# The read of one group of eight moved from GpSimd to VectorE, its states kept in PSUM, and the replicated buffers turned by halves

## The chip, the cores and the metric

The kernel runs on one core of one Trainium2 chip. The metric is the device time of one launch in microseconds. Five engines work side by side: TensorE (PE, with its weight loads PEld), VectorE (DVE), ScalarE (ACT), GpSimd (POOL) and SyncE (SP), which issues most of the transfers.

## The reference

For each of 32 sequences of 256 time steps and 128 features the kernel computes a selective state-space block and then a mixture-of-experts block, both with a layer norm ahead and a residual. Cut to what matters here, for each sequence:

```
uo = norm(x) @ W_in.T ; u, o = halves of uo ; u = silu(conv(u))       # 256 channels
g = u @ W_gate.T -> delta_lo (64), b (16), c (16)
delta = softplus(delta_lo @ W_delta.T + bias) ; A = -exp(A_log)
h[t] = exp(A * delta[t]) * h[t-1] + (delta[t] * u[t]) * b[t]          # 256 channels x 16 states
y[t] = sum over states of h[t] * c[t] ; y = (y + D * u) * silu(o) ; x = x + y @ W_out.T
x = x + experts(norm(x))    # router, top 2 of 8, silu(x wg) * (x wu) wd, and a shared expert
```

## The kernel before

**The scan.** One sequence has 256 channels x 16 states. They are cut into eight groups (`q` from 0 to 7; `half` of the channels is `q // 4`, four states `g` are `q % 4`), and each group is a tile of 128 partitions x 4 blocks x 256 time steps, so 128x1024. For each group:

- `decays` on ScalarE (L451): four Exp activations from the replicated delta (`rep[..., 0, :]`) into `decay_ps`, a PSUM tensor of two slots used in turn (`at % 2`);
- `inject_group` on GpSimd (L384): the replicated delta times u, times b, into `inject` (four slots);
- `scan` on VectorE (L648): one scan along the 1024 columns, decays and injections in, `state` (three slots) out. Column 0 of each block in `decay_ps` is kept at zero, which starts each block anew;
- `read_group` on GpSimd (L393): `state` times c into `read` (three slots);
- `sum_states` on TensorE (L856): four matmuls with `sum_sel` that add the products over states into `y_ps`.

**What feeds it.** `dd` holds delta (copied by ScalarE, L536, from PSUM) and delta times u (VectorE, L780); eight DMAs of SP (L330), four for each half of the channels, replicate it to `rep`. A buffer `rep[n % 2]` holds both halves, so there are four halves of space in all. b and c come by two DMAs into `bc`.

**The order.** The kernel is a software pipeline: `steps(body)` calls, on each engine, `body(k, on)` for k from -3 to 34, and in step k the scan of sequence k runs beside the expert block of sequence k-2 (`f`), the first layer norm and convolution of sequence k+2, and delta and replication of sequence k+1. Each engine runs its own program in order, written out by hand, and waits on semaphores. VectorE has, in a step: scan(0), scan(1), the small operations of the router, scan(2), the low part of xnT (L769), scan(3), scan(4), then `dd` (L780, which waits for `delta_mm`, the matmul L991), then `gated_up(4)` and so on. GpSimd has injects 1 to 3, reads 0 and 1, inject 4, reads 2, 3 and 4, injects 5 to 7, inject 0 of the next sequence, the small `shift` (L414), reads 5 to 7. TensorE's `ups(4, f)` (L1007, its matmuls at L873) waits for `dd_done`, since `delta_ps` and the bank of `ups(4)` are the same PSUM bank. ScalarE copies `dd` only when VectorE's L780 is done:

```
act.wait_ge(du_done, n + 1)
...
act.copy(dd[:, :, 0, :], delta_ps).then_inc(dd_done, 1)
...
pe.wait_ge(dd_done, k + 2)
...
ups(4, f)
```

Of the kernel before, what the change touches and what calls it, by code (L numbers as in the profile page):

```python
# [5 lines left out]
ALU = mybir.AluOpType  # L6
# [5 lines left out]
P = 128  # L12
# [7 lines left out]
CB = P // GS  # L20
# [18 lines left out]
SCALE = 2.5  # L39
LOW = 32  # L40

RX, RU, RI, RS, RR = 5, 3, 4, 3, 3


GATE_BANK = [0, 2, 1, 0, 1, 1, 0]
# [5 lines left out]

def rows(chunk):
    return LAST if chunk == NSH - 1 else P


def comb_chunks(i):
# [4 lines left out]
def build(nc, x, W_in, conv_w, conv_b, W_gate, W_delta, delta_bias, A_log, Dskip, W_out,  # L61
          gate_w, w_gate, w_up, w_down, sw_gate, sw_up, sw_down, out):
    with ExitStack() as ctx:
        def sb(name, shape, dt=F32):
            return ctx.enter_context(nc.sbuf_tensor(name, shape, dt))

        def sem(name):
            return ctx.enter_context(nc.semaphore(name))
# [1 line left out]
        features = sb("features", [P, CHUNKS, T])  # L70
        state = sb("state", [P, RS, JB, T])
        read = sb("read", [P, RR, JB, T])
        rep = [sb(f"rep{i}", [P, HALVES * JB, 2, T]) for i in range(2)]

        scratch = features[:].rearrange("p c t -> p (c t)")
        wconv_rows = scratch[:, 0:1024].rearrange("p (c k d) -> p c k d", c=HALVES, k=TAPS)
# [148 lines left out]
        inject_done = sem("inject_done")  # L225
        state_done = sem("state_done")
        read_done = sem("read_done")
        sum_done = sem("sum_done")
        y_taken = sem("y_taken")

# [52 lines left out]
        def count(value):  # L283
            return max(value, 0)
# [13 lines left out]
        @block.sync  # L298
        def _(sp):
            sp.dma_start(x_in[0][:], x_t[0]).then_inc(x_loaded[0], 16)  # L300
            for to, source in setup_loads:
                sp.dma_start(to, source).then_inc(w_loaded, 16)

            def body(k, on):
                if on(1):
                    n = k + 1
                    sp.wait_ge(bc_out, 16 * (n + 1))
                    sp.wait_ge(inject_done, count(GROUPS * k))
                    sp.wait_ge(read_done, count(GROUPS * k))
                    for which, landed in enumerate((b_in, c_in)):  # L310
                        rows_of = bc_dram[:, which, :, :].rearrange("s g t -> s (g t)")
                        sp.dma_start(bc[n % 2][:, which, :, :].rearrange("p g t -> p (g t)"),
                                     rows_of.unsqueeze(0).broadcast_to([CB, GS, SG * T])).then_inc(landed, 16)
                if on(-3):
                    n = k - 3
                    sp.wait_ge(result_done, n + 1)
                    sp.dma_start(out_t[n], result[n % 2][:]).then_inc(stored[n % 2], 16)
                if on(4):

                    n = k + 4  # L320
                    sp.wait_ge(x1_done, count(n - RX + 1))
                    sp.dma_start(x_in[n % RX][:], x_t[n]).then_inc(x_loaded[n % RX], 16)
                if on(1):
                    n = k + 1
                    sp.wait_ge(dd_done, n + 1)
                    sp.wait_ge(decay_done, count(GROUPS * k))
                    for half in range(HALVES):
                        for j in range(JB):
                            source = dd[j * CB:(j + 1) * CB, half, :, :].rearrange("c w t -> c (w t)")
                            sp.dma_start(rep[n % 2][:, half * JB + j, :, :].rearrange("p w t -> p (w t)"),  # L330
                                         source.unsqueeze(1).broadcast_to([CB, GS, 2 * T])).then_inc(rep_in[half], 16)
# [12 lines left out]
        def _(pool):  # L344
# [30 lines left out]
            def body(k, on):  # L375
                def inject_group(n, q):
                    half, g = divmod(q, SG)
                    at = GROUPS * n + q
                    pool.wait_ge(rep_in[half], 16 * JB * (n + 1))
                    pool.wait_ge(b_in, 16 * (n + 1))  # L380
                    pool.wait_ge(state_done, count(at - RI + 1))
                    du_all = rep[n % 2][:, half * JB:(half + 1) * JB, 1, :]
                    b_all = bc[n % 2][:, 0, g, :].unsqueeze(1).broadcast_to([P, JB, T])
                    pool.tensor_tensor(inject[:, at % RI], du_all, b_all, ALU.mult).then_inc(inject_done, 1)  # L384

                def read_group(n, q):
                    half, g = divmod(q, SG)
                    at = GROUPS * n + q
                    pool.wait_ge(c_in, 16 * (n + 1))
                    pool.wait_ge(state_done, at + 1)  # L390
                    pool.wait_ge(sum_done, count(at - RR + 1))
# [12 lines left out]

                injects(1, 2, 3)
                reads(0, 1)
                injects(4)
                reads(2, 3, 4)
                injects(5, 6, 7)
                if on(1):  # L410
                    inject_group(k + 1, 0)
                if on(3) or on(-1):
                    pool.wait_ge(ln_rstd, k + 4)
                    pool.tensor_tensor(shift[:], neg_mean[:], rstd[:], ALU.mult).then_inc(ln_shift, 1)  # L414
                reads(5, 6, 7)
# [4 lines left out]
        def _(act):  # L420
# [14 lines left out]
            def body(k, on):  # L435
# [8 lines left out]
                def decays(n, q):  # L444
                    half, g = divmod(q, SG)
                    at = GROUPS * n + q
                    act.wait_ge(rep_in[half], 16 * JB * (n + 1))
                    act.wait_ge(state_done, count(at - 1))
                    for j in range(JB):
                        col = (g * HALVES + half) * JB + j  # L450
                        last = act.activation(decay_ps[:, at % 2, j, 1:T], rep[n % 2][:, half * JB + j, 0, 1:T], ACT.Exp,  # L451
                                              scale=neg_a[:, col:col + 1])
                    last.then_inc(decay_done, 1)

# [145 lines left out]
        def _(dve):  # L600
# [39 lines left out]
            def body(k, on):  # L640
                f = k - 2

                def scan(q):
                    at = GROUPS * k + q
                    dve.wait_ge(decay_done, at + 1)
                    dve.wait_ge(inject_done, at + 1)
                    dve.wait_ge(read_done, count(at - RS + 1))
                    dve.tensor_tensor_scan(state[:, at % RS].rearrange("p j t -> p (j t)"),  # L648
                                           decay_ps[:, at % 2].rearrange("p j t -> p (j t)"),
                                           inject[:, at % RI].rearrange("p j t -> p (j t)"), 0.0,  # L650
                                           ALU.mult, ALU.add).then_inc(state_done, 1)

                def gated_up(p):
                    at = PAIRS * f + p
# [171 lines left out]
        def _(pe):  # L826
# [18 lines left out]
            def body(k, on):  # L845
                f = k - 2

                def sum_states(n, q):
                    half, g = divmod(q, SG)
                    at = GROUPS * n + q  # L850
                    if g == 0:
                        pe.matmul(y_ps, skip[:, half, :], u[n % RU][:, half, :], start=True, stop=False,
                                  skip_group_check=True)
                    pe.wait_ge(read_done, at + 1)
                    for j in range(JB):
                        last = pe.matmul(y_ps[j * CB:(j + 1) * CB, :], sum_sel[:], read[:, at % RR, j, :],  # L856
                                         start=False, stop=(g == SG - 1), skip_group_check=True)
                    last.then_inc(sum_done, 1)

# [263 lines left out]
```

## Time and profile before

| what | value |
|---|---|
| median of 3 runs | 1453.29 us (1452.8 to 1456.53) |
| the profiled execution, its own time | 1453.74 us |
| its span from first to last instruction | 1451.6 us |
| busy share of the span | PE 88%, PEld 65%, DVE 72%, ACT 74%, POOL 84% |
| a step in the steady part | about 41.5 us |
| TensorE's granted clock, mean | 0.961 of full speed |

An engine's busy share is an average over the whole span; start and end, where the pipeline fills and empties, are in it. The time of a launch is a little longer than the span in the trace. Times in the rows are in us from the start of the span, and the name in brackets behind a row is what ended the engine's idle time before it.

### The profile page before, as it was taken

The page shows a single profiled execution, that of the slowest core. Times are in us where ns is not written, and L with a number is a line of the kernel's source. Part 1 is how long each engine was busy: PE and PEld are TensorE (multiplying, and loading weights), DVE is VectorE, ACT ScalarE, POOL GpSimd, SP SyncE. Part 2 cuts the span into 40 slices and gives each one's busy share as a digit, 9 for nine tenths or more (in the row PEclk, how much of TensorE's full clock was granted, in tenths as well). Part 3 has the DMA queues.
Part 4 walks back from the last instruction along what each step waited for, and adds up shares of the span by engine and source line. Part 5 has one row for each costly group of instructions (what it writes and reads, how often), then busy time and mean ns, then how long its engine had stood idle before and what let it go on. Part 6 is the DMA issues. An engine that isn't in the chain of part 4 may idle for free.

```text
span 1451.6 us, 26176 instructions
## 1 busy us (share of the span) xinstructions
PE 1273.9 (88%) x9203; PEld 950.7 (65%) x9203; DVE 1042.5 (72%) x1664; ACT 1080.1 (74%) x2219; POOL 1219.0 (84%) x568
## 2 busy tenths in 40 slices
PE   3455999999999999999999999999999999998888
PEld 2223766777667667776676677766766777665677
DVE  2245778877777788777777887777778877776753
ACT  3777778777877787778777877787778777876642
POOL 3299898898889988988899889888998898899920
PEclk8667999999999999999999999999999999999989
DMA  3433322333333223333332233333322333233000
GB/s 102 103 89 84 92 67 69 95 96 92 74 86 95 65 70 96 96 93 75 84 94 66 70 96 96 92 74 85 95 65 69 96 97 92 69 83 89 7 5 8
DMA packets 71486, 115.08 MB, mean 79 GB/s; under 512 B 8174, under 2 KB 30396, under 8 KB 71356
## 3 DMA queue, kind: packets, MB, share of 16 engines
q1 hardware_dynamic: 67180, 110.71, 30.2%
q10 hardware_dynamic: 4176, 2.70, 0.6%
q8 instruction: 73, 1.20, 0.3%
q14 instruction: 57, 0.47, 0.1%
HBM read 41.04 MB, written 5.24 MB: 32 GB/s over the span
## 4 chain that ended last, share of the span: by engine, by line
PE 34%; DVE 22%; ACT 17%; issue 16%; POOL 1%; DVEq 0%; SPq 0%; DMA 0%; ACTq 0%; POOLq 0%
DVE state L648 11%; PE work_ps L864 10%; PE work_ps L873 10%; ACT decay_ps L451 6%; DVE features L666 5%; PE acc_ps L898 4%; ACT L483 3%; ACT L504 3%; PE acc_ps L856 3%; ACT L548 3%; PE work_ps L1081 2%; PE work_ps L997 2%; PE work_ps L927 2%; ACT u L526 2%; DVE features L658 2%
## 5 line engine op out<-in xcount | busy, mean ns | idle before, releaser
L393 POOL TENSOR_TENSOR read<-state,bc 128x1024 f32<-128x1024 f32 x256 | 605.6, 2379 | 93.0 <-DVE state L648 87.6
L384 POOL TENSOR_TENSOR inject<-rep,bc 128x1024 f32<-128x1024 f32 x256 | 604.4, 2385 | 52.2 <-DMA rep<-dd 52.2
L648 DVE TENSOR_TENSOR_SCAN state<-decay_ps,inject 128x1024 f32<-128x1024 f32 x256 | 580.9, 2280 | 48.3 <-ACT decay_ps L451 29.5
L451 ACT ACTIVATE decay_ps<-rep,neg_a 128x255 f32<-128x255 f32 x1024 | 423.5, 462 | 14.6 <-DVE state L648 5.5
L442 ACT ACTIVATE g_silu<-work_ps 128x512 f32<-128x512 f32 x224 | 133.9, 598 | 204.3 <-PE work_ps L864 204.0
L658 DVE TENSOR_TENSOR features<-g_silu,work_ps 128x512 f32<-128x512 f32 x224 | 151.6, 678 | 147.5 <-PE work_ps L873 107.5
L898 PE MATMUL acc_ps<-ffn_down,features 128*128 128x128 f32 (+1 forms) x1792 | 252.5, 284 | 0.0
L898 PEld LDWEIGHTS acc_ps<-ffn_down,features 128*128 128x128 f32 (+1 forms) x1792 | 217.2, 191 | 30.1 <-issue 12.3
L864 PE MATMUL work_ps<-xn2T_part,ffn_gate 128*128 128x256 f32 x1344 | 210.9, 294 | 2.5 <-ACT combT L499 1.8
L873 PE MATMUL work_ps<-xn2T_part,ffn_up 128*128 128x256 f32 x1344 | 207.7, 291 | 1.4 <-ACT dd L536 1.4
L856 PE MATMUL acc_ps<-read,sum_sel 128*32 128x256 f32 x2048 | 168.3, 401 | 37.8 <-POOL read L393 37.6
L873 PEld LDWEIGHTS work_ps<-xn2T_part,ffn_up 128*128 128x128 f32 x1344 | 180.5, 195 | 27.4 <-ACT dd L536 13.6
L864 PEld LDWEIGHTS work_ps<-xn2T_part,ffn_gate 128*128 128x128 f32 x1344 | 180.6, 196 | 17.4 <-issue 13.1
L666 DVE TENSOR_TENSOR features<-features,work_ps 128x512 f32<-128x512 f32 (+1 forms) x192 | 113.9, 630 | 18.1 <-PE work_ps L885 18.1
L979 PE MATMUL work_ps<-xnT_part,wconv 128*128 128x256 f32 x768 | 103.2, 292 | 26.7 <-DVE xnT_part L769 26.7
L979 PEld LDWEIGHTS work_ps<-xnT_part,wconv 128*128 128x128 f32 x768 | 96.5, 194 | 37.2 <-DVE xnT_part L769 36.4
L856 PEld LDWEIGHTS acc_ps<-read,sum_sel 128*32 128x32 f32 x2048 | 40.8, 109 | 110.0 <-POOL read L393 49.2
L885 PE MATMUL work_ps<-combT,csel 40*128 40x256 f32 x352 | 87.4, 334 | 2.0 <-DVE features L658 2.0
L474 ACT ACTIVATE gate<-work_ps 128x512 f32<-128x512 f32 x32 | 19.1, 596 | 66.8 <-PE work_ps L927 66.8
L885 PEld LDWEIGHTS work_ps<-combT,csel 40*128 40x128 f32 x352 | 53.4, 185 | 20.4 <-DVE features L658 2.8
L927 PE MATMUL work_ps<-xnT_part,wo 128*128 128x256 f32 x192 | 32.3, 305 | 34.4 <-DVE features L658 30.7
L780 DVE TENSOR_TENSOR dd<-work_ps,u 128x512 f32<-128x512 f32 x32 | 22.1, 691 | 48.9 <-PE work_ps L991 48.9
(134 smaller groups left out, 1398.5 us busy)
## 6 DMA issues: line engine op xcount, KB each, us to landing
rep<-dd SPq DMA_DIRECT2D x256, 256.0 KB, 4.8
bc<-bc_rows SPq DMA_DIRECT2D x64, 512.0 KB, 4.8
x_in<-in_L_attn_x_dram SPq DMA_DIRECT2D x32, 128.0 KB, 2.2
out_dram<-result SPq DMA_DIRECT2D x32, 128.0 KB, 1.8
bc_rows<-g_sb SPq DMA_DIRECT2D x32, 32.0 KB
state<-in_L_ffn_w_gate_dram ACTq DMA_DIRECT2D x1, 704.0 KB, 4.4
read<-in_L_ffn_w_up_dram ACTq DMA_DIRECT2D x1, 704.0 KB, 5.9
ffn_down<-in_L_ffn_w_down_dram ACTq DMA_DIRECT2D x1, 704.0 KB, 7.1
```

The lines of the kernel that those rows point to most:

```text
L384: pool.tensor_tensor(inject[:, at % RI], du_all, b_all, ALU.mult).then_inc(inject_done, 1)
L393: pool.tensor_tensor(read[:, at % RR], state[:, at % RS], c_all, ALU.mult).then_inc(read_done, 1)
L451: last = act.activation(decay_ps[:, at % 2, j, 1:T], rep[n % 2][:, half * JB + j, 0, 1:T], ACT.Exp, scale=neg_a[:, col:col + 1])
L648: dve.tensor_tensor_scan(state[:, at % RS].rearrange("p j t -> p (j t)"), decay_ps[:, at % 2].rearrange("p j t -> p (j t)"), inject[:, at ...
L658: dve.tensor_tensor(features[:, 2 * p:2 * p + 2, :].rearrange("p c t -> p (c t)"), g_silu[p % 2][:], banks[UP_BANK[p]][:], ALU.mult).then_ ...
L666: dve.tensor_tensor(to, to, banks[COMB_BANK[i]][:, 0:len(chunks) * T], ALU.mult).then_inc(hc_done, 1)
L856: last = pe.matmul(y_ps[j * CB:(j + 1) * CB, :], sum_sel[:], read[:, at % RR, j, :], start=False, stop=(g == SG - 1), skip_group_check=True)
L864: last = pe.matmul(banks[GATE_BANK[p]][:, side * T:(side + 1) * T], ffn_gate[w][:, chunk * P:(chunk + 1) * P], xn2T_parts[n % 2][d][:], st ...
L873: last = pe.matmul(banks[UP_BANK[p]][:, side * T:(side + 1) * T], ffn_up[w][:, chunk * P:(chunk + 1) * P], xn2T_parts[n % 2][d][:], start= ...
L885: last = pe.matmul(banks[COMB_BANK[i]][:, at * T:(at + 1) * T], csel[:, (chunk - NSH) * P:(chunk - NSH + 1) * P], combT[:], start=True, st ...
L898: last = pe.matmul(down_ps[:, j * DIM:(j + 1) * DIM], features[0:r, chunk, j * P:(j + 1) * P], ffn_down[0:r, chunk, :], start=fresh and j ...
L979: last = pe.matmul(conv_ps[:, half * T:(half + 1) * T], wconv[w][:, half, tap, :], xnT_parts[d][:, tap:tap + T], start=(w + d + tap == 0), ...
```

## The change

Group 4 (`OWN`), the fifth of each sequence, is treated apart. Its scan writes its states in place over its decays in `decay_ps`, not into `state`. VectorE, not GpSimd, multiplies them by c into a new tile `read_own` (128x1024), and then sets column 0 of the slot's four blocks to zero again with a memset. `sum_states` of this group takes `read_own`. The decays of group 6, which use the same slot, wait for the memset. GpSimd reads only seven groups, and the slots of `state` and `read` are counted over these seven (`others`, `of_others`). The replicated buffers are three of one half each, in turn, in place of two of both halves; the DMAs of each half wait for the decays and injections that used its buffer.

```
-RX, RU, RI, RS, RR = 5, 3, 4, 3, 3
+RX, RU, RI, RS, RR, RP = 5, 3, 4, 3, 3, 3
+OWN = 4
+OTHERS = GROUPS - 1
...
+def others(n, q):
+    return OTHERS * n + (q if q < OWN else q - 1)
+def of_others(at):
+    n, q = divmod(at, OTHERS)
+    return GROUPS * n + (q if q < OWN else q + 1)
...
-        rep = [sb(f"rep{i}", [P, HALVES * JB, 2, T]) for i in range(2)]
+        read_own = sb("read_own", [P, JB, T])
+        rep = [sb(f"rep{i}", [P, JB, 2, T]) for i in range(RP)]
...
                     sp.wait_ge(dd_done, n + 1)
-                    sp.wait_ge(decay_done, count(GROUPS * k))
                     for half in range(HALVES):
+                        sp.wait_ge(decay_done, count(SG * (HALVES * n + half - RP + 1)))
+                        sp.wait_ge(inject_done, count(SG * (HALVES * n + half - RP + 1)))
...
-                reads(2, 3, 4)
+                reads(2, 3)
...
-                    act.wait_ge(state_done, count(at - 1))
+                    if q == OWN + 2:
+                        act.wait_ge(decay_zero, n + 2)
+                    else:
+                        act.wait_ge(state_done, count(at - 1))
...
-                    dve.wait_ge(read_done, count(at - RS + 1))
-                    dve.tensor_tensor_scan(state[:, at % RS].rearrange("p j t -> p (j t)"),
-                                           decay_ps[:, at % 2].rearrange("p j t -> p (j t)"),
+                    decays = decay_ps[:, at % 2].rearrange("p j t -> p (j t)")
+                    if q == OWN:
+                        to = decays
+                    else:
+                        dve.wait_ge(read_done, count(others(k, q) - RS + 1))
+                        to = state[:, others(k, q) % RS].rearrange("p j t -> p (j t)")
+                    dve.tensor_tensor_scan(to, decays,
                                            inject[:, at % RI].rearrange("p j t -> p (j t)"), 0.0,
                                            ALU.mult, ALU.add).then_inc(state_done, 1)
+
+                def read_own_group():
+                    dve.wait_ge(c_in, 16 * (k + 1))
+                    dve.wait_ge(state_done, GROUPS * k + OWN + 1)
+                    dve.wait_ge(sum_done, count(GROUPS * (k - 1) + OWN + 1))
+                    c_all = bc[k % 2][:, 1, OWN % SG, :].unsqueeze(1).broadcast_to([P, JB, T])
+                    dve.tensor_tensor(read_own[:], decay_ps[:, OWN % 2], c_all, ALU.mult).then_inc(read_own_done, 1)
+                    dve.wait_ge(read_own_done, k + 1)
+                    dve.memset(decay_ps[:, OWN % 2, :, 0:1], 0.0).then_inc(decay_zero, 1)
...
                 if on(0):
                     scan(4)
+                    read_own_group()
...
-                    pe.wait_ge(read_done, at + 1)
+                    if q == OWN:
+                        pe.wait_ge(read_own_done, n + 1)
+                        products = read_own
+                    else:
+                        pe.wait_ge(read_done, others(n, q) + 1)
+                        products = read[:, others(n, q) % RR]
```

VectorE's order in the middle of a steady step, before (L648 is a scan, L769 the low part of xnT, L780 the product for `dd`):

```order
L761 TENSOR_TENSOR comb_parts<-work_ps,comb_parts 128x2x8 [waits comb_split]
L648 SCALAR_TENSOR_TENSOR state<-decay_ps,inject 128x1024 [waits read_done,inject_done,decay_done]
L769 TENSOR_TENSOR xnT_part<-work_ps,xnT_part 128x256 [waits xnT_high]
L648 SCALAR_TENSOR_TENSOR state<-decay_ps,inject 128x1024 [waits read_done,inject_done,decay_done] x2
L780 TENSOR_TENSOR dd<-work_ps,u 128x2x256 [waits rep_in1,rep_in0,delta_mm]
L658 TENSOR_TENSOR features<-g_silu,work_ps 128x512 [waits down_mm,ffu_mm,silu_done]
```

The same place of the changed kernel, whose lines are numbered anew (L675 is the scan, L684 the product with c, L686 the memset, L816 the product for `dd`):

```order
L796 TENSOR_TENSOR comb_parts<-work_ps,comb_parts 128x2x8 [waits comb_split]
L675 SCALAR_TENSOR_TENSOR state<-decay_ps,inject 128x1024 [waits read_done,inject_done,decay_done]
L804 TENSOR_TENSOR xnT_part<-work_ps,xnT_part 128x256 [waits xnT_high]
L675 SCALAR_TENSOR_TENSOR state<-decay_ps,inject 128x1024 [waits read_done,inject_done,decay_done]
L675 SCALAR_TENSOR_TENSOR decay_ps<-decay_ps,inject 128x1024 [waits inject_done,decay_done]
L684 TENSOR_TENSOR read_own<-decay_ps,bc 128x1024 [waits sum_done,state_done,c_in]
L686 MEMSET decay_ps 128x4 [waits read_own_done]
L816 TENSOR_TENSOR dd<-work_ps,u 128x2x256 [waits rep_in1,rep_in0,delta_mm]
```

Two instructions now stand between scan(4) and the product for `dd`, and each of them waits for the one ahead of it.

GpSimd's order over one step, before (L384 is an inject, L393 a read):

```order
L384 TENSOR_TENSOR inject<-rep,bc 128x1024 [waits state_done,b_in,rep_in1]
L393 TENSOR_TENSOR read<-state,bc 128x1024 [waits sum_done,state_done,c_in] x3
L384 TENSOR_TENSOR inject<-rep,bc 128x1024 [waits state_done,b_in,rep_in1] x3
L384 TENSOR_TENSOR inject<-rep,bc 128x1024 [waits state_done,b_in,rep_in0]
L414 TENSOR_TENSOR shift<-neg_mean,rstd 128x4 [waits ln_rstd]
```

And of the changed kernel (L403 is an inject, L412 a read):

```order
L403 TENSOR_TENSOR inject<-rep,bc 128x1024 [waits state_done,b_in,rep_in1]
L412 TENSOR_TENSOR read<-state,bc 128x1024 [waits sum_done,state_done,c_in] x2
L403 TENSOR_TENSOR inject<-rep,bc 128x1024 [waits state_done,b_in,rep_in1] x3
L403 TENSOR_TENSOR inject<-rep,bc 128x1024 [waits state_done,b_in,rep_in0]
L433 TENSOR_TENSOR shift<-neg_mean,rstd 128x4 [waits ln_rstd]
```

The third of the reads behind inject 4 is gone, and the three injects and all behind them follow one operation sooner.

## Rows read from the trace of the kernel before

**Rows 1.** The page's part 1, busy time and share of each engine.

```profile
PE 1273.9 (88%) x9203; PEld 950.7 (65%) x9203; DVE 1042.5 (72%) x1664; ACT 1080.1 (74%) x2219; POOL 1219.0 (84%) x568
```

**Rows 2.** Busy time by stretch: length, PE, PEld, DVE, ACT, POOL, clock, DMA.

```profile
815.00:1230.00 415.00, 387.01 (x2872) 290.42 (x2871) 320.83 (x510) 326.86 (x680) 377.70 (x171) 1.00 0.33 84
```

**Rows 3.** The page's part 4, shares of the chain that ended last, by engine.

```profile
PE 34%; DVE 22%; ACT 17%; issue 16%; POOL 1%; DVEq 0%; SPq 0%; DMA 0%; ACTq 0%; POOLq 0%
```

**Rows 4.** Timeline of GpSimd over one step: start, length, operation, idle before.

```profile
633.87 2.36 POOL L384 TENSOR_TENSOR inject<-rep,bc 128x1024 f32<-128x1024 f32 x1 [0.60 <-DMA rep<-dd]
...
639.46 2.37 POOL L393 TENSOR_TENSOR read<-state,bc 128x1024 f32<-128x1024 f32 x1 [0.74 <-DVE state L648]
...
660.50 7.22 POOL L393 TENSOR_TENSOR read<-state,bc 128x1024 f32<-128x1024 f32 x3 [1.25 <-DVE state L648]
667.66 7.08 POOL L384 TENSOR_TENSOR inject<-rep,bc 128x1024 f32<-128x1024 f32 x3
675.40 2.37 POOL L384 TENSOR_TENSOR inject<-rep,bc 128x1024 f32<-128x1024 f32 x1 [0.66 <-DMA rep<-dd]
```

**Rows 5.** The chain in order of time, same step: start, length, what.

```profile
658.07 2.30 DVE state L648
...
666.56 1.10 PE work_ps L997 x4
667.66 0.91 PE work_ps L873 x6
...
675.13 0.04 DVE state L648
```

**Rows 6.** Timeline of all engines from 665 to 668.3, same step.

```profile
662.79 2.26 DVE L648 TENSOR_TENSOR_SCAN state<-decay_ps,inject 128x1024 f32<-128x1024 f32 x1
...
666.23 0.69 DVE L780 TENSOR_TENSOR dd<-work_ps,u 128x512 f32<-128x512 f32 x1 [1.18 <-PE work_ps L991]
...
666.95 0.58 ACT L536 COPY dd<-work_ps 128x512 f32<-128x512 f32 x1
...
667.59 0.77 PEld L873 LDWEIGHTS work_ps<-xn2T_part,ffn_up 128*128 128x128 f32 x6 [0.36 <-ACT dd L536]
```

**Rows 7.** Waits over the whole span: us in total, times, longest.

```profile
DVE dd L780 <- PE work_ps L991: 48.9, 32, 5.6
...
PEld work_ps L873 <- ACT dd L536: 13.6, 29, 3.0
```

**Rows 8.** Timeline of VectorE, same step: a shorter product, and three operations in a row.

```profile
648.36 0.42 DVE L672 TENSOR_TENSOR y_gated<-acc_ps,gate 128x256 f32<-128x256 f32 x1 [0.23 <-PE acc_ps L856]
...
657.76 0.17 DVE L759 CAST comb_parts<-work_ps 128x16 fp32r<-128x16 f32 x1
657.97 0.17 DVE L761 TENSOR_TENSOR comb_parts<-work_ps,comb_parts 128x16 fp32r<-128x16 f32 x1
658.07 2.29 DVE L648 TENSOR_TENSOR_SCAN state<-decay_ps,inject 128x1024 f32<-128x1024 f32 x1
```

**Rows 9.** The instructions of one line: the memset of decay_ps, min/median/max ns.

```profile
L638 DVE MEMSET decay_ps<- x1: 65/65/65, 21.3 to 21.3; 128x8 f32 x1
```

**Rows 10.** Timeline of VectorE: a product written to PSUM, and one written to SBUF.

```profile
644.55 0.29 DVE L813 TENSOR_TENSOR work_ps<-logit,work_ps 128x128 f32<-128x128 f32 x1
644.75 0.28 DVE L815 TENSOR_TENSOR ahead<-logit,work_ps 128x128 f32<-128x128 f32 x1
```

**Rows 11.** Timeline of SP's queue, same step.

```profile
667.56 8.92 SPq L330 DMA_DIRECT2D rep<-dd  x8
```

**Rows 12.** Timelines of the first and the last steps, VectorE's L780.

```profile
87.81 0.69 DVE L780 TENSOR_TENSOR dd<-work_ps,u 128x512 f32<-128x512 f32 x1 [4.49 <-PE work_ps L991]
...
1330.04 0.69 DVE L780 TENSOR_TENSOR dd<-work_ps,u 128x512 f32<-128x512 f32 x1 [1.51 <-PE work_ps L991]
```

**Rows 13.** Timeline of GpSimd at the end of step 0.

```profile
96.80 2.35 POOL L384 TENSOR_TENSOR inject<-rep,bc 128x1024 f32<-128x1024 f32 x1 [1.94 <-DMA rep<-dd]
```

**Rows 14.** Timeline of ScalarE, same step: the decays of group 3.

```profile
658.04 1.66 ACT L451 ACTIVATE decay_ps<-rep,neg_a 128x255 f32<-128x255 f32 x4
```

More of the change, by code:

```diff
@@ L227, in build @@
         read_done = sem("read_done")
+        read_own_done = sem("read_own_done")
         sum_done = sem("sum_done")
@@ L308, in body @@
                     sp.wait_ge(inject_done, count(GROUPS * k))
-                    sp.wait_ge(read_done, count(GROUPS * k))
+                    sp.wait_ge(read_done, count(OTHERS * k))
+                    sp.wait_ge(read_own_done, count(k))
                     for which, landed in enumerate((b_in, c_in)):
@@ L325, in body @@
                     sp.wait_ge(dd_done, n + 1)
-                    sp.wait_ge(decay_done, count(GROUPS * k))
                     for half in range(HALVES):
+                        sp.wait_ge(decay_done, count(SG * (HALVES * n + half - RP + 1)))
+                        sp.wait_ge(inject_done, count(SG * (HALVES * n + half - RP + 1)))
                         for j in range(JB):
                             source = dd[j * CB:(j + 1) * CB, half, :, :].rearrange("c w t -> c (w t)")
-                            sp.dma_start(rep[n % 2][:, half * JB + j, :, :].rearrange("p w t -> p (w t)"),
+                            sp.dma_start(rep[(HALVES * n + half) % RP][:, j, :, :].rearrange("p w t -> p (w t)"),
                                          source.unsqueeze(1).broadcast_to([CB, GS, 2 * T])).then_inc(rep_in[half], 16)
@@ L381, in inject_group @@
                     pool.wait_ge(state_done, count(at - RI + 1))
-                    du_all = rep[n % 2][:, half * JB:(half + 1) * JB, 1, :]
+                    du_all = rep[(HALVES * n + half) % RP][:, :, 1, :]
                     b_all = bc[n % 2][:, 0, g, :].unsqueeze(1).broadcast_to([P, JB, T])
@@ L387, in read_group @@
                     half, g = divmod(q, SG)
[L388 removed]
+                    at = others(n, q)
                     pool.wait_ge(c_in, 16 * (n + 1))
[L390 to L391 removed]
+                    pool.wait_ge(state_done, GROUPS * n + q + 1)
+                    pool.wait_ge(sum_done, count(of_others(at - RR) + 1))
                     c_all = bc[n % 2][:, 1, g, :].unsqueeze(1).broadcast_to([P, JB, T])
@@ L447, in decays @@
                     act.wait_ge(rep_in[half], 16 * JB * (n + 1))
-                    act.wait_ge(state_done, count(at - 1))
+                    if q == OWN + 2:
+                        act.wait_ge(decay_zero, n + 2)
+                    else:
+                        act.wait_ge(state_done, count(at - 1))
                     for j in range(JB):
                         col = (g * HALVES + half) * JB + j
-                        last = act.activation(decay_ps[:, at % 2, j, 1:T], rep[n % 2][:, half * JB + j, 0, 1:T], ACT.Exp,
+                        last = act.activation(decay_ps[:, at % 2, j, 1:T], rep[(HALVES * n + half) % RP][:, j, 0, 1:T], ACT.Exp,
                                               scale=neg_a[:, col:col + 1])
@@ L853, in sum_states @@
                                   skip_group_check=True)
-                    pe.wait_ge(read_done, at + 1)
+                    if q == OWN:
[4 more added lines that the diff above has]
+                        products = read[:, others(n, q) % RR]
                     for j in range(JB):
-                        last = pe.matmul(y_ps[j * CB:(j + 1) * CB, :], sum_sel[:], read[:, at % RR, j, :],
+                        last = pe.matmul(y_ps[j * CB:(j + 1) * CB, :], sum_sel[:], products[:, j, :],
                                          start=False, stop=(g == SG - 1), skip_group_check=True)
```

## The prediction

> **What bounds the kernel now.** I read the busy shares first, then the steady part by itself, then the chain that ended last, then one step engine by engine.
>
> Over the whole span TensorE is busy 88% and GpSimd 84% [rows 1]. In a steady stretch of 415 us, ten steps, PE is busy 387.0, POOL 377.7, ACT 326.9 and DVE 320.8 us, at the full clock [rows 2]. A step is 675.40 - 633.87 = 41.5 us, read between two injects of the same place [rows 4]. So GpSimd is busy 37.8 of 41.5 us, and by shares alone one would say that it is nearly the limit, and that one 2.36 us read taken from it must pay.
>
> The chain says otherwise: GpSimd has 1% of it; PE has 34%, DVE 22%, ACT 17% [rows 3]. The timeline of GpSimd shows why: its 3.7 us of idle time in a step end, each time, on a scan of VectorE or on a DMA of `rep` [rows 4]. In the steady part I found no engine that waits for GpSimd long enough to move its own work. GpSimd follows; it does not lead.
>
> What leads is a loop through three engines. In one step [rows 5]: VectorE's scan(2) at 658.07, ScalarE's table loads and u, TensorE's g matmuls (L997) at 666.56, `ups(4)` (L873) at 667.66, the gate and up matmuls behind it, ScalarE's last silu, table load and decays, scan(5) at 675.13; from there scans, router and expert matmuls lead back to the next scan(2). TensorE works without a gap from `ups(4)` to the last silu's matmuls, so a late `ups(4)` makes all of it late.
>
> The place to look at is just ahead of `ups(4)` [rows 6]. scan(4) ends at 662.79 + 2.26 = 665.05. VectorE idles 1.18 us for the matmul L991 and runs L780 from 666.23 to 666.92. ScalarE's copy (L536) starts at 666.95, 0.03 us later, and ends at 667.53. The weight load of `ups(4)` starts at 667.59, ended by that copy. L997's matmuls end at 667.66 by the chain, and matmuls overlap their forerunner by about 0.07 us, so the matmul was free to start at 667.59 too. **The two paths into `ups(4)` are level: what makes L780 late makes the step late.** It is so in nearly all steps: PEld's wait for this copy is counted 29 times [rows 7].
>
> **The change part by part.**
>
> *GpSimd loses one read of about 2.36 us in each step.* It comes behind inject 4. Injects 5 to 7, from 667.66 to 674.74, move forward by 2.4 us, but the next inject waits for `rep`, already now until 675.40 [rows 4]. Its transfers start at 667.56, when `dd` is done [rows 11], and don't move forward. So the 2.4 us become idle time there, 3.0 us in place of 0.66. Gain: nothing. In step 0, where the pipeline fills, the inject of the same place already waits 1.94 us [rows 13]; nothing there either.
>
> *VectorE gains three things between scan(4) and L780*: the wait for the scan, the product, the wait for the product and the memset. 1.18 us of idle time cover them; the question is whether this is enough.
> - The product, 128x1024, one operand in PSUM: no row has this size. 128x256 takes 0.42 [rows 8], 128x512 takes 0.69 [rows 6], so 0.27 for each 256 columns and 0.69 + 2 x 0.27 = 1.23 for 1024. Upper bound two of 512, 1.38.
> - A wait for the operation just ahead: L759 ends at 657.93 and L761, which waits for it, starts at 657.97, a gap of 0.04 [rows 8]. Operations that don't wait start before the forerunner ends: L761 ends at 658.14, the scan behind it starts at 658.07, 0.10 us after L761 started. Two such waits are added: 0.04 each, upper bound 0.10.
> - The memset: 0.065 us for 8 columns [rows 9], here 4. L780 doesn't wait for it and starts between 0.03 and 0.10 us after it; the nearest row has 0.10 [rows 8] behind a longer operation, and I take 0.09. Upper bound 0.17, the length of a small operation [rows 8].
>
> Sum: 665.05 + 0.04 + 1.23 + 0.04 + 0.09 = 666.45. L780 started at 666.23, so it is **0.22 us late**. Its output releases the copy, the copy `ups(4)` and the DMAs of `rep`. What is late next is the whole loop, 0.22 us in each step.
>
> *How many steps.* L780 waits 32 times for 48.9 us [rows 7]. Step 0 has 4.49 us of cover, the last one (step 30) 1.51 [rows 12], more than the 1.40 added. Steps 2 to 29 are alike, 28 of them. 28 x 0.22 = 6.2 us. Lower bound of the sum: with the gap behind scan(4) and the product alone, 665.05 + 0.04 + 1.23 = 666.32, 0.09 late, 2.5 us. Upper bound: 665.13 + 0.10 + 1.38 + 0.10 + 0.17 = 666.88, 0.65 late, 18 us (the scan's 0.08 is below).
>
> *The scan into PSUM, in place*: a product of 128 columns written to PSUM takes 0.29, one written to SBUF 0.28 [rows 10]. I take no difference; by this row 1024 columns could cost 0.08. No row shows a scan written to PSUM.
>
> *The wait of decays 6 for the memset*: the memset ends at about 666.4, the decays start at 675 or later. Covered by 8 us. *scan(4) no longer waits for a read*: it did not wait before. *PE's `sum_states` of group 4*: product ready at 666.3, taken at 674. Free.
>
> *The three halves of `rep`.* Half 0 of the next sequence goes to the buffer of the sequence before's second half, long read. Half 1 goes where the running sequence's half 0 lay: it needs decays 0 to 3 and injects 0 to 3. Decays 3 end at 659.70 [rows 14], the DMAs start at 667.56 [rows 11] and those of half 1 some 4 us later. Cover 8 us and more; cost nothing. Without that cover the replication would wait, and inject 0 and read 5 behind it.
>
> *A rule against my sum.* The rows show that a wait costs: a start 0.04 us after the forerunner's end in place of 0.07 before it [rows 8], 0.11 us for each of two waits, and this is my 0.22 us. The Trainium skill, page "VectorE: DVE Perf Modes", section "The DRAIN you can't avoid", says that between VectorE operations "the semaphore costs nothing extra". By it the sum would be 666.23 and the delay nothing. The row shows the contrary, though on small operations; a rival below takes this in.
>
> **The total.** 1453.74 (the profiled execution's own time) + 6.2 = 1459.9. That execution is 0.45 us above the median of the runs, so against the median: 1459.5 us, 0.4% slower.
>
> **The rivals.** A measurement of this kernel tells a difference from none at about 0.3%, 4.4 us.
> - *The added work just fits.* If the waits overlap as operations without waits do, L780 starts within 0.05 us of its old time and the time stays at 1453.3 to 1455. For it: the margin is a fifth of a microsecond and every term is short. Against: the gap of 0.04 us. With it go the lower bound above (0.09 us, 1455.8) and all delays up to 0.155 us: 35%.
> - *The scan in place is dear.* 2.26 us for 1024 columns is 2.2 ns each, two reads or so per column. If reading and writing one PSUM bank made it half slower, scan(4) would grow by 1.1 us, L780 be 1.3 us late, the time 1453 + 28 x 1.3 = 1490. Against: the 0.01 us of [rows 10]. With milder forms, up to the upper bound of 18 us and beyond: 11%.
> - *Faster: GpSimd is the limit after all.* It is busy 91% of a step [rows 2]. If the scans that it waits for themselves wait for it through a path that the chain hides, a step could shrink by up to the 2.4 us removed: 28 x 2.4 = 67 us, 1386. It decides once the loop through the scans is shorter than GpSimd's own 37.8 us; the loop would have to lose 3.7 us first, and the change takes nothing from it. 6%.
> - *The forecast*, L780 0.155 to 0.4 us late in each step, 1457.7 to 1464.5: 48%.
>
> **The numbers.** Slower by over 0.3%: 48 + 11 = 59%. Within 0.3%: 35%. Faster: 6%. The range from 1453 to 1467 holds the forecast, the case that fits, and the milder half of the dear scan; outside are the 6% faster and the dearest scans, and what is shifted by chance at the lower edge. The forecast's own range is 1457.7 to 1464.5.
>
> **What would show it.** Right: the step is 41.7 us; the product's row has about 1.23 us; VectorE's idle time ahead of the `dd` product, 1.18 before, is gone, while PEld's wait for the copy of `dd` grows by 0.2 us a time; GpSimd's wait for `rep` grows from 0.66 to about 3 us; GpSimd's busy time falls by 32 x 2.4 = 76 us with no gain in time. Wrong: some idle time left ahead of the `dd` product (it fits), a scan to PSUM well over 2.28 us (dear), or a step under 41.5 us (GpSimd). It would also be wrong if TensorE could start `ups(4)` with slack that the modelled ends of matmuls hide.

## The result and the profile after

The changed kernel takes 1461.48 us in the median (16 runs, 1457.69 to 1467.27), the kernel before on the same chips 1454.9 us (16 runs, 1450.6 to 1460.43). The ratio is 1.0052, 95% interval 1.0035 to 1.0069: slower by half a per cent, which is 7.6 us; the two medians differ by 6.6. 1459.5 us and 0.4% were forecast.

Between launches of one kernel the time spreads over 10 us, more than the effect, and in the traces it is mostly the filling and the last steps that vary. A finer measure is the length of one step in the steady part, from one `dd` product of VectorE to the next. Inside the trace of the changed kernel 26 of the 27 steps from 3 to 29 agree within 0.03 us and one is 0.34 longer; in that of the kernel before all but two agree within 0.05, and these are 0.23 and 0.39 longer. The median over these steps is 41.473 us before and 41.766 us after, 0.29 us more. This is the number that the experiments below compare.

The page of the changed kernel, part 1:

```profile
PE 1277.7 (88%) x9203; PEld 951.6 (65%) x9203; DVE 1084.3 (74%) x1728; ACT 1078.0 (74%) x2219; POOL 1144.2 (78%) x536
```

GpSimd lost 75 us of work, VectorE got 42, and the span went from 1451.6 to 1459.1. The timeline of the place just ahead of `ups(4)`, which answers to [rows 6] (L675 is the scan, L684 the product with c, L686 the memset, L816 the product for `dd`, L558 ScalarE's copy, L914 `ups(4)`):

```profile
623.96 2.27 DVE L675 TENSOR_TENSOR_SCAN decay_ps<-decay_ps,inject 128x1024 f32<-128x1024 f32 x1
...
626.33 1.23 DVE L684 TENSOR_TENSOR read_own<-decay_ps,bc 128x1024 f32<-128x1024 f32 x1
...
627.63 0.06 DVE L686 MEMSET decay_ps<- 128x4 f32 x1
627.70 0.69 DVE L816 TENSOR_TENSOR dd<-work_ps,u 128x512 f32<-128x512 f32 x1
...
628.42 0.59 ACT L558 COPY dd<-work_ps 128x512 f32<-128x512 f32 x1 [0.25 <-DVE dd L816]
...
629.06 0.77 PEld L914 LDWEIGHTS work_ps<-xn2T_part,ffn_up 128*128 128x128 f32 x6 [0.65 <-ACT dd L558]
629.06 0.98 PE L914 MATMUL work_ps<-xn2T_part,ffn_up 128*128 128x256 f32 x6 [0.22 <-ACT dd L558]
```

Read it from the top. scan(4) ends at 626.23. The `dd` product starts at 627.70, 1.46 us later by the unrounded times, where it was 666.23 - 665.05 = 1.18 before. VectorE no longer waits for the matmul that makes delta (L991 before); its 1.18 us of idle time are used up and 0.28 us more. ScalarE now waits 0.25 us for the product, and TensorE, which had no gap here, 0.22 us for the copy. The step is longer by 0.29.

The waits over the whole span say the same, as answers to [rows 7]:

```profile
POOL inject L403 <- DMA rep<-dd: 132.7, 32, 26.6
...
PEld work_ps L914 <- ACT dd L558: 21.5, 29, 3.0
...
ACT dd L558 <- DVE dd L816: 11.9, 32, 1.5
PE work_ps L914 <- ACT dd L558: 7.9, 29, 1.4
```

TensorE itself has a wait of 7.9 us in 29 steps, 0.27 each in the mean, but 0.22 in nearly all of them and 1.4 in one. And GpSimd's wait for `rep` is 132.7 us, where it was 52.2 before. The first line is that of the kernel before, the second one step now, against [rows 4], where it was 0.66:

```profile
POOL inject L384 <- DMA rep<-dd: 52.2, 32, 28.1
...
637.05 2.37 POOL L403 TENSOR_TENSOR inject<-rep,bc 128x1024 f32<-128x1024 f32 x1 [3.17 <-DMA rep<-dd]
```

The read that was taken from GpSimd has become idle time in front of the next inject. The three instructions that had no row before, with min/median/max in ns:

```profile
L675 DVE TENSOR_TENSOR_SCAN state<-decay_ps,inject x224: 2262/2281/2292, 65.8 to 1394.7; 128x1024 f32<-128x1024 f32 x112
L675 DVE TENSOR_TENSOR_SCAN decay_ps<-decay_ps,inject x32: 2272/2272/2299, 79.8 to 1376.3; 128x1024 f32<-128x1024 f32 x32
```

```profile
L684 DVE TENSOR_TENSOR read_own<-decay_ps,bc x32: 1224/1225/1226, 82.2 to 1378.7; 128x1024 f32<-128x1024 f32 x32
```

```profile
L686 DVE MEMSET decay_ps<- x32: 62/62/62, 83.5 to 1380.0; 128x4 f32 x32
```

The product takes 1.225 us, the memset 0.06. The scan in place takes 2.272 us, less than the median of those into SBUF; but scan(4) of the kernel before, in the same place, took 2.262 ([rows 6] has it as 2.26), so the way into PSUM costs 0.01 us at most.

### The profile page after: what moved, and what is told of

It is laid out like the page before. It is cut to its first block and busy times, and to the rows that moved or that the text cites. A ratio compares the mean times of both kernels' runs of the same rounds, so it can differ in the third digit from the quotient of the medians.

```text
span 1459.1 us, 26272 instructions
## 1 busy us (share of the span) xinstructions
PE 1277.7 (88%) x9203; PEld 951.6 (65%) x9203; DVE 1084.3 (74%) x1728; ACT 1078.0 (74%) x2219; POOL 1144.2 (78%) x536
## 5 line engine op out<-in xcount | busy, mean ns | idle before, releaser
L403 POOL TENSOR_TENSOR inject<-rep,bc 128x1024 f32<-128x1024 f32 x256 | 604.3, 2383 | 132.7 <-DMA rep<-dd 132.7
L412 POOL TENSOR_TENSOR read<-state,bc 128x1024 f32<-128x1024 f32 x224 | 530.5, 2377 | 92.5 <-DVE state L675 87.5
L675 DVE TENSOR_TENSOR_SCAN state<-decay_ps,inject 128x1024 f32<-128x1024 f32 x224 | 511.1, 2283 | 44.2 <-ACT decay_ps L473 29.3
L914 PE MATMUL work_ps<-xn2T_part,ffn_up 128*128 128x256 f32 x1344 | 208.3, 292 | 7.9 <-ACT dd L558 7.9
L914 PEld LDWEIGHTS work_ps<-xn2T_part,ffn_up 128*128 128x128 f32 x1344 | 181.1, 196 | 35.5 <-ACT dd L558 21.5
L897 PE MATMUL acc_ps<-read,sum_sel 128*32 128x256 f32 x1792 | 148.4, 404 | 36.3 <-POOL read L412 35.9
L897 PEld LDWEIGHTS acc_ps<-read,sum_sel 128*32 128x32 f32 x1792 | 35.7, 109 | 98.3 <-POOL read L412 47.5
L675 DVE TENSOR_TENSOR_SCAN decay_ps<-decay_ps,inject 128x1024 f32<-128x1024 f32 x32 | 72.8, 2274 | 3.8 <-POOL inject L403 3.8
```

The source lines that it names most:

```text
L675: dve.tensor_tensor_scan(to, decays, inject[:, at % RI].rearrange("p j t -> p (j t)"), 0.0, ALU.mult, ALU.add).then_inc(state_done, 1)
L897: last = pe.matmul(y_ps[j * CB:(j + 1) * CB, :], sum_sel[:], products[:, j, :], start=False, stop=(g == SG - 1), skip_group_check=True)
L914: last = pe.matmul(banks[UP_BANK[p]][:, side * T:(side + 1) * T], ffn_up[w][:, chunk * P:(chunk + 1) * P], xn2T_parts[n % 2][d][:], start= ...
```

## The experiments

The theory: the loop through `dd`, its copy and `ups(4)` sets the time; the product and the memset stand ahead of `dd` and make it late by what exceeds 1.18 us. The rivals: the turn of `rep`, the scan into PSUM or other waits cost it; GpSimd's lighter work is worth something that another loss hides; the loop has slack that takes part of a delay. Steps are medians over steps 3 to 29 of one trace. Ratios are to runs of the kernel before that were made beside each kernel, not to the first row: their median is 1453.01 us for `e1` to `e4`, 1455.78 for `e5` to `e8`, and `e9` and `e10` have a single one of 1452.02. One run's time can't tell half a per cent; where there is only one, the step is what counts.

| kernel | step, us | time, us | ratio to before |
|---|---|---|---|
| before | 41.47 | 1454.9 | 1 |
| changed | 41.77 | 1461.48 | 1.0052 [1.0035, 1.0069] |
| `e1_dd_first` | 41.48 | 1455.74 | 1.0015 [1.0, 1.003] |
| `e2_memset_behind` | 41.52 | 1450.69, one run | |
| `e3_no_product` | 41.47 | 1455.69 | 1.0013 [0.9995, 1.003] |
| `e4_gpsimd_refilled` | 41.75 | 1459.36, one run | |
| `e5_rep_alone` | 41.47 | 1451.57, one run | |
| `e6_product_twice` | 42.88, then 44.37 | 1529.67, one run | |
| `e7_scan1_later` | 40.51 | 1428.74 | 0.9811 [0.9784, 0.9838] |
| `e8_both` | 40.51 | 1422.08 | 0.9782 [0.975, 0.9813] |
| `e9_scan1_and_change` | 40.79 | 1431.23, one run | |
| `e10_three_blocks` | 41.49 | 1451.72, one run | |

**The added work behind `dd`, in place of ahead of it.**

```
                 if on(0):
                     scan(4)
-                    read_own_group()
...
                     dve.tensor_tensor(dd[:, :, 1, :], delta_ps, u[n % RU][:], ALU.mult).then_inc(du_done, 1)
+                if on(0):
+                    read_own_group()
```

> The changed kernel with the product with c and the memset of group 4 placed behind the product for dd, where VectorE idles 1.74 us for ups(4). Theory (the added work delays dd): the added 1.35 us fits into that idle time, dd is on time again, the step falls from 41.77 back to 41.47 us and the time to that of the kernel before, ratio 0.998 to 1.002. Rival 1 (the turn of rep, the scan into PSUM or the waits of other engines cost it): the step stays near 41.77, ratio 1.005. Rival 2 (GpSimd's shorter work is worth something once VectorE's delay is gone): step under 41.4, ratio under 0.998.

The timeline of VectorE in this kernel (L815 is the `dd` product):

```profile
622.30 0.69 DVE L815 TENSOR_TENSOR dd<-work_ps,u 128x512 f32<-128x512 f32 x1 [1.18 <-PE work_ps L1033]
...
622.91 1.21 DVE L684 TENSOR_TENSOR read_own<-decay_ps,bc 128x1024 f32<-128x1024 f32 x1
...
624.20 0.06 DVE L686 MEMSET decay_ps<- 128x4 f32 x1
...
624.74 0.69 DVE L693 TENSOR_TENSOR features<-g_silu,work_ps 128x512 f32<-128x512 f32 x1 [0.48 <-issue]
```

`dd` has its 1.18 us of idle time ahead of it again, the same work fits behind it with 0.48 us to spare, and the step is 41.48. Everything else of the change is still in this kernel, so nothing else of it lengthens the step. The ratio is 1.0015, and its interval just reaches 1, so the times would allow a loss of up to 0.3%; the step shows none. In this trace the last `dd` product starts at 1327.01 of a span of 1456.4, so 129 us lie behind it, where before it was 122. The page's granted clock, 40 slices in tenths, ends in 9978 where that of before ends in 9989:

```profile
PEclk9767999999999999999999999999999999999978
```

So the last steps ran at a lower clock in this execution; the steady steps are not touched by that. No gain is to be seen either: the second rival falls.

**Only the memset behind `dd`.**

```
                     dve.tensor_tensor(read_own[:], decay_ps[:, OWN % 2], c_all, ALU.mult).then_inc(read_own_done, 1)
-                    dve.wait_ge(read_own_done, k + 1)
-                    dve.memset(decay_ps[:, OWN % 2, :, 0:1], 0.0).then_inc(decay_zero, 1)
...
                     dve.tensor_tensor(dd[:, :, 1, :], delta_ps, u[n % RU][:], ALU.mult).then_inc(du_done, 1)
+                if on(0):
+                    dve.wait_ge(read_own_done, k + 1)
+                    dve.memset(decay_ps[:, OWN % 2, :, 0:1], 0.0).then_inc(decay_zero, 1)
```

> The changed kernel with only the memset (and its wait for the product) placed behind the product for dd; the product with c stays ahead of it. If a VectorE operation that waits for the one ahead costs more than one that doesn't, the product for dd starts before the product with c ends: some 0.2 us sooner than in the changed kernel, the step is 41.52 to 41.58 us. If, as the rival has it, the wait costs nothing extra, only the memset's own 0.06 us is saved and the step is 41.70.

The timeline of VectorE (L814 is the `dd` product, L817 the memset):

```profile
618.66 2.27 DVE L675 TENSOR_TENSOR_SCAN decay_ps<-decay_ps,inject 128x1024 f32<-128x1024 f32 x1
...
621.02 1.23 DVE L684 TENSOR_TENSOR read_own<-decay_ps,bc 128x1024 f32<-128x1024 f32 x1
...
622.16 0.68 DVE L814 TENSOR_TENSOR dd<-work_ps,u 128x512 f32<-128x512 f32 x1
...
622.85 0.06 DVE L817 MEMSET decay_ps<- 128x4 f32 x1
```

From the start of the product to the start of `dd` it is 1.14 us, against 1.37 in the changed kernel. So a memset of 0.06 us that waits for its forerunner costs 0.23 us there, 0.17 of it beyond its own length. The step is 41.52, at the lower end of what was expected; `dd` is 1.23 us behind the scan, 0.04 late, and the step is longer by 0.05.

**No product at all, the ceiling of the change.**

```
-                    dve.tensor_tensor(read_own[:], decay_ps[:, OWN % 2], c_all, ALU.mult).then_inc(read_own_done, 1)
+                    dve.memset(read_own[:, 0, 0:4], 0.0).then_inc(read_own_done, 1)
```

> The changed kernel without the product with c of group 4 (a memset of four columns of read_own stands in its place, read_own is zero, so group 4 adds nothing to y): GpSimd does seven reads, VectorE the scan in place, two memsets. This is the most that the change could bring. Theory (GpSimd is not on the path): added work about 0.35 us is under VectorE's cover of 1.18, the step is 41.47 and the ratio 0.998 to 1.002. Rival (GpSimd's 2.4 us a step are worth something): step under 41.3, ratio under 0.995.

The step is 41.47 and the ratio 1.0013. With one read of GpSimd's eight gone and almost nothing in its place, the kernel is no faster than before. What the change set out from, 2.4 us a step off GpSimd, is worth nothing by itself. The same place in this trace (L685 is the memset that stands for the product, L687 the one that waits for it):

```profile
664.22 2.27 DVE L676 TENSOR_TENSOR_SCAN decay_ps<-decay_ps,inject 128x1024 f32<-128x1024 f32 x1
666.62 0.06 DVE L685 MEMSET read_own<- 128x4 f32 x1
666.75 0.06 DVE L687 MEMSET decay_ps<- 128x4 f32 x1
667.66 0.69 DVE L817 TENSOR_TENSOR dd<-work_ps,u 128x512 f32<-128x512 f32 x1 [0.85 <-PE work_ps L1033]
```

VectorE idles 0.85 us for the matmul again. The second memset starts 0.075 us after the end of the first, as it does behind the product of 1024 columns in the changed kernel.

**GpSimd's work put back.**

```
                 reads(2, 3)
+                if on(0):
+                    pool.wait_ge(spare_done, k)
+                    pool.tensor_tensor(spare[:], state[:, others(k, 3) % RS],
+                                       bc[k % 2][:, 1, 3, :].unsqueeze(1).broadcast_to([P, JB, T]),
+                                       ALU.mult).then_inc(spare_done, 1)
```

The later scans and the loads of b and c wait for the spare product too.

> The changed kernel with one more 128x1024 product on GpSimd where the read of group 4 stood (group 3 once more, to a spare tile, that nobody reads), so that GpSimd works as much as before the change. Theory: GpSimd's wait for rep falls from about 3 us to 0.6 and nothing else moves, step 41.77 as in the changed kernel. Rival (the lighter GpSimd gave something back that hid a larger loss): step over 41.85.

A steady step of it, length, PE, PEld, DVE, ACT and POOL busy:

```profile
543.27:585.02 41.75, 38.73 (x287) 29.01 (x287) 33.38 (x54) 32.61 (x69) 37.74 (x18) 1.00 0.34 84
```

And one of the changed kernel:

```profile
585.94:627.70 41.76, 38.78 (x287) 29.06 (x287) 33.38 (x54) 32.62 (x69) 35.11 (x17) 1.00 0.34 84
```

GpSimd is busy 37.74 in place of 35.11 us and the step does not move: the median is 41.75. GpSimd's wait for `rep` in a step, 3.36 us in the median of the changed kernel, is 1.04 here, not quite the 0.6 that was expected.

**The three halves of `rep` alone, in the kernel before.**

```
-                    sp.wait_ge(decay_done, count(GROUPS * k))
                     for half in range(HALVES):
+                        sp.wait_ge(decay_done, count(SG * (HALVES * n + half - RP + 1)))
+                        sp.wait_ge(inject_done, count(SG * (HALVES * n + half - RP + 1)))
```

> The kernel before with the replicated buffers as three halves in turn and nothing else of the change. Theory: its waits are met 8 us ahead, step 41.47 us, span 1451 to 1453. Rival (the turn of rep costs part of the loss): step over 41.5.

41.47 us, as before. This part of the change costs nothing. The span, 1449.4 us, lies below the 1451 to 1453 expected; those of the kernel before, run beside it, went from 1449.1 to 1456.7.

**The product twice.**

```
+                    dve.wait_ge(spare_done, k)
+                    dve.tensor_tensor(spare[:], decay_ps[:, OWN % 2], c_all, ALU.mult).then_inc(spare_done, 1)
                     dve.tensor_tensor(read_own[:], decay_ps[:, OWN % 2], c_all, ALU.mult).then_inc(read_own_done, 1)
```

> The changed kernel with the product with c of group 4 made twice on VectorE, the first time to a spare tile. Theory (from where the cover is used up, every us ahead of the dd product is a us of the step): the second product adds its 1.225 us less the overlap of about 0.08, plus nothing else; step 41.77 + 1.15 = 42.9 us, span about 1491. Rival (the loop has slack elsewhere that takes part of it): step under 42.6.

The first five full steps (3 to 7) are 42.88 to 42.89 us, as expected. From step 8 on they are 44.37. The timeline: first `ups(4)` (L918) in step 3, then a later step (L820 is the `dd` product):

```profile
211.69 0.97 PE L918 MATMUL work_ps<-xn2T_part,ffn_up 128*128 128x256 f32 x6 [1.35 <-ACT dd L560]
...
646.76 1.22 DVE L688 TENSOR_TENSOR read_own<-decay_ps,bc 128x1024 f32<-128x1024 f32 x1
...
648.05 0.06 DVE L690 MEMSET decay_ps<- 128x4 f32 x1
648.12 0.69 DVE L820 TENSOR_TENSOR dd<-work_ps,u 128x512 f32<-128x512 f32 x1
...
649.48 1.49 PE L918 MATMUL work_ps<-xn2T_part,ffn_up 128*128 128x256 f32 x6 [1.35 <-ACT dd L560]
```

And the same kernel's busy time by stretch, granted clock third from the right:

```profile
646.00:648.00 2.00, 1.64 (x6) 0.57 (x4) 1.97 (x2) 1.44 (x4) 2.00 (x2) 1.00 0.00 0
648.00:650.00 2.00, 0.65 (x4) 0.52 (x4) 0.75 (x2) 0.85 (x2) 2.00 (x2) 0.92 0.00 0
650.00:652.00 2.00, 2.00 (x14) 0.96 (x13) 0.69 (x1) 0.00 (x0) 2.00 (x2) 0.50 0.60 80
652.00:654.00 2.00, 2.00 (x13) 2.00 (x14) 0.42 (x1) 0.55 (x1) 1.10 (x1) 0.73 0.96 182
```

TensorE idles 1.35 us for the copy of `dd`, starts again, and then its granted clock is 0.50 of full speed, 1.2 in place of 2.4 GHz, for 3.4 us: the end of the second stretch, all of the third and about half of the fourth. The six matmuls of `ups(4)` take 1.49 in place of 0.98 us, and those behind them are slower too. So the delay itself acted one to one (steps 3 to 7 are 1.41 us longer than before, for a `dd` that comes 2.59 us behind the scan in place of 1.19), and with the low clock another 1.5 us came on top. In step 3 the same wait of 1.35 us left the clock at full speed and the six matmuls at 0.97 us, as the first row shows. The span, 1527.9 us, missed the expected 1491 because of it.

**Three quarters of the product.**

```
-                    c_all = bc[k % 2][:, 1, OWN % SG, :].unsqueeze(1).broadcast_to([P, JB, T])
-                    dve.tensor_tensor(read_own[:], decay_ps[:, OWN % 2], c_all, ALU.mult).then_inc(read_own_done, 1)
+                    c_all = bc[k % 2][:, 1, OWN % SG, :].unsqueeze(1).broadcast_to([P, 3, T])
+                    dve.tensor_tensor(read_own[:, 0:3], decay_ps[:, OWN % 2, 0:3], c_all, ALU.mult).then_inc(read_own_done, 1)
```

> The changed kernel with the product with c over three of the four blocks of group 4, 768 columns (the fourth block of read_own stays zero, so its channels lack group 4's part of y). The product takes 0.96 in place of 1.225 us, so dd is late by 0.29 - 0.27 = 0.02 us. Theory (a cover of 1.18 us and a slope of one behind it): step 41.47 to 41.51 us. Rival (a fixed price for having the product there at all): step over 41.6.

The product takes 0.96 us, the `dd` product starts 1.19 us behind the scan as it did before, and the step is 41.49. There is no fixed price for having the product there; below the cover it is free.

**scan(1) behind `gated_up(2)`, in the kernel before.** This is a place on the loop that the change doesn't touch.

```
-                if on(0):
-                    scan(1)
                 pairs(2)
+                if on(0):
+                    scan(1)
```

> The kernel before with scan(1) placed behind gated_up(2) on VectorE and nothing of the change. In the loop TensorE's L927 waits 1.07 us for gated_up(2), which stands behind scan(1). Theory (the loop sets the time, and this is on it): L927 starts about 1 us sooner, step 40.4 to 40.8 us, ratio 0.975 to 0.985, GpSimd is busy 93% of a step and still does not decide. Rival (GpSimd or another engine holds the step): step over 41.2.

TensorE's timeline of the kernel before, L927 behind VectorE's `gated_up(2)`:

```profile
653.14 0.97 PE L927 MATMUL work_ps<-xnT_part,wo 128*128 128x256 f32 x6 [1.07 <-DVE features L658]
```

And of this one:

```profile
638.65 0.88 PE L873 MATMUL work_ps<-xn2T_part,ffn_up 128*128 128x256 f32 x6
639.37 0.87 PE L927 MATMUL work_ps<-xnT_part,wo 128*128 128x256 f32 x6
...
642.12 0.64 PE L856 MATMUL acc_ps<-read,sum_sel 128*32 128x256 f32 x8 [0.32 <-POOL read L393]
```

L927 follows its forerunner at once. The step is 40.51, 0.96 us shorter, the time 1.9% less, ratio 0.9811. An exchange of two neighbours on the loop brings three times what the change cost. In the last row TensorE waits 0.32 us for a read of GpSimd; over the span there are 41 such waits, where there were 12 before: in the shorter step GpSimd begins to be waited for. The median hides what this does in single steps. In steps 5 and 19 the inject that waits for `rep` starts 10.60 and 10.22 us behind the `dd` product, where 9.3 is usual, and the steps are 0.48 and 0.11 us longer than the median. TensorE in step 5:

```profile
262.25 0.64 PE L856 MATMUL acc_ps<-read,sum_sel 128*32 128x256 f32 x8 [1.09 <-POOL read L393]
```

So a late replication now reaches TensorE by way of GpSimd; in step 5 of the kernel before, where it was 9.56 us, the step was no longer than the others. What made it late was not looked for.

**The same in the changed kernel, with the added work behind `dd`.**

> The changed kernel with the product with c and the memset behind the dd product, and scan(1) behind gated_up(2). If GpSimd decides nothing even in the shorter loop, the step is that of the kernel with scan(1) later alone, within 0.05 us. Rival (in the shorter loop the 2.4 us taken from GpSimd begin to pay): step 0.1 us or more below that one's.

Step 40.51, ratio 0.9782 [0.975, 0.9813], not to be told from the other's 0.9811 [0.9784, 0.9838]. Both beat the kernel before by about 2%; that the lighter GpSimd adds something to it is not shown. TensorE waits for a read as often as there, 40 times against 41. In this trace no steady step is longer by 0.1 us, but its replications were less late too (9.67 and 9.63 us in steps 5 and 19), so it doesn't settle this. The read that TensorE waits for in a shorter step is that of group 0, and the read that was removed stands ahead of the wait for `rep`, which takes its time up in this kernel as in the others.

**The same in the changed kernel as it is.**

> The changed kernel as it is, product and memset ahead of the dd product, with only scan(1) placed behind gated_up(2). Theory (two places of one loop, whose prices add): the step is that of scan(1) later alone, 40.51 us, plus the change's 0.29 us: 40.80. Rival (the price depends on the rest of the step): further than 0.1 us from 40.80.

Step 40.79, 0.28 us over `e7_scan1_later`. The two places are parts of one loop and their prices add.

## Why the prediction was right

The direction, the place and the mechanism were right, point by point.

- *GpSimd leads nothing.* Shown three ways: its read left out gives nothing (`e3_no_product`), its work put back costs nothing (`e4_gpsimd_refilled`), and its wait for `rep` took up the 2.4 us, as forecast (0.66 to 3.17 us in a step). This holds for the step of 41.5 us; in the one of 40.5 single steps are lengthened by way of GpSimd (`e7_scan1_later`).
- *`dd` late, `ups(4)` late, the step late, one to one.* The lateness of `dd` behind the scan (medians, from 1.19 us before) against the lengthening of the step: 0.00 and 0.01 (`e10_three_blocks`), 0.04 and 0.05 (`e2_memset_behind`), 0.27 and 0.29 (changed), 1.40 and 1.41 (`e6_product_twice`, before the clock fell). The 0.01 that most pairs differ by is the length that the scan in place has more.
- *The cover of 1.18 us.* Right. With the work moved out of it the loss is gone (`e1_dd_first`).
- *The size, 0.22 us a step forecast, 0.29 measured.* The product was 1.225 us for 1.23. The mis-sized term is the wait for the operation ahead, put at 0.04 us: by the unrounded times it was 0.09 behind the scan and 0.075 behind the product. From the start of the memset to that of `dd` it was 0.07 for 0.09. Together 0.05 + 0.035 - 0.02 - 0.005 = 0.06, which makes 0.28 of 0.22, and the scan in place, taken as no longer, adds its 0.01. I had read 0.04 from small operations, where it is true. The length of the operation ahead doesn't explain the larger gap: in `e3_no_product` a memset has the same 0.075 behind another of four columns. The upper bound given, 0.10, held.
- *28 steps.* 28 x 0.29 = 8.1 us by the step; the spans of the two traces differ by 7.5, the ratio gives 7.6, the medians 6.6, and 6.2 was forecast. The interval of the ratio allows 5 to 10 us, so the times alone don't tell 6.2 from 8.1; that the median came within 2 us of the forecast is in part chance, and it is the step that shows the term was too small.
- *The rule against the sum.* The Trainium skill, "VectorE: DVE Perf Modes", section "The DRAIN you can't avoid", has the semaphore cost nothing extra. Here an operation that waits for the one just ahead costs 0.17 us beyond its length (`e2_memset_behind`). By that rule the change would have been free. The measurement that the Trainium skill gives there is of eight copies, with a semaphore after each or only after the last; whether each copy waited for the one ahead it doesn't say. What is paid here is such a wait, and the measurement decides.
- *`rep` in halves, the scan in place, the memset wait of decays 6: free.* `e5_rep_alone` shows the first, the rows of L675 the second (but for 0.01 us); the third is seen only in that `e1_dd_first`, where the memset comes later still, loses nothing.

The rival that "the added work just fits" failed by 0.28 us of 1.46, less than the two waits, the overlap that they forbid and the memset together (some 0.17, 0.16 and 0.06 us). The prediction gave it 35%, and the kernel `e2_memset_behind` shows how near it was.

## What to carry to other kernels

An engine that is busy 91% of a step need not hold it: look at what ends its idle times, and at whether anybody waits for it. Before you move work to another engine, find the idle time that is to take it, measure it against the work with its waits included, and see what stands behind it in that engine's order; here the same work is free one place later. Keep an operation that waits for its direct forerunner out of such a gap, or put an independent one between them.

## What the runs showed of the hardware

- A VectorE operation that waits for the one just ahead started 0.034 us after its end behind small operations (L759 and L761), 0.09 when the product waited for the scan, and 0.075 when a memset waited, behind a product of 1024 columns and behind a memset of four columns alike (changed kernel, `e3_no_product`). One that doesn't wait mostly started 0.07 to 0.09 us before that end. What sets the size of the gap stays open.
- A scan of 1024 columns that writes in place over its own input in PSUM takes 2.272 us; into SBUF it took 2.262 in the same place of the kernel before, 2.281 in the median of all places.
- A wait of 1.35 us of TensorE in each step was followed by half the granted clock for 3.4 us, and the step was 1.5 us longer than the wait alone had made it. In five early steps with the same wait the clock stayed full and the step shows no such loss. Why it set in at step 8 stays open.
- Single steady steps are 0.2 to 0.4 us longer than the others, at most two in a trace but for `e7_scan1_later`, which has more; in the one of the changed kernel VectorE idles 0.36 us between memset and `dd` with no releaser in the profile. The cause was not looked for.
